# More landing places for the tiles of adj, and the context loaded from GpSimd's queue

## What is computed

```python
h = relu(layernorm(x))
# layer 0: hyperbolic layer; scales per node come from norms of h and of h @ W.T
xt = logmap0(proj(mobius_add(mobius_matvec(W, h), bias)))   # 4096 x 128
s  = adj @ xt                                               # phase 1
x  = x + proj(expmap0(relu(logmap0(proj(expmap0(s))))))
h  = relu(layernorm(x))
# layer 1: attention over the edges of adj
left, right = (context @ W_common.T) @ w_left + b_left, (...) @ w_right + b_right
e = leaky_relu(left[:, None] + right[None, :], 0.2)         # only where adj > 0
x = x + relu(softmax(e) @ h)                                # phase 2
```

## Time and profile before

| | us |
|---|---|
| three runs | 608.92, 609.44, 620.27 |
| median | 609.44 |
| the profiled execution | 609.72 |
| its span | 607.9 |
| start of the first multiplication of phase 1 | 57.84 |
| last copy of the support (phase 1 has ended) | 317.2 |

### The profile page before, as it was taken

How to read it: one execution, slowest core, us unless ns; L and a number is a source line. 1 busy time by engine, 2 the same in 40 slices (tenths; PEclk the granted TensorE clock), 3 DMA queues, 4 the chain that set the end, 5 groups by cost and what they waited for, 6 DMA issues and landing times.

```text
span 607.9 us, 8702 instructions
## 1 busy us (share of the span) xinstructions
PE 500.0 (82%) x2695; PEld 317.0 (52%) x2695; DVE 520.0 (86%) x980; ACT 420.8 (69%) x554; POOL 271.0 (45%) x323
## 2 busy tenths in 40 slices
PE   0731999997999979996984667798989899999995
PEld 0620444332444334432422445687878787887874
DVE  3797898878788788865778999999999999999994
ACT  1965886674757466753658773888888888989871
POOL 4840037989698978672448974201011111111100
PEclk9985999999899989997995788999999999999999
DMA  6999899999999999999950100001010101011010
GB/s 156 218 224 185 156 259 292 299 285 293 245 269 297 278 266 268 295 251 206 269 113 17 36 0 17 20 19 37 18 36 18 35 17 35 17 35 35 0 35 17
DMA packets 157181, 84.59 MB, mean 139 GB/s; under 512 B 7344, under 2 KB 155056, under 8 KB 157152
## 3 DMA queue, kind: packets, MB, share of 16 engines
q1 hardware_dynamic: 88768, 47.20, 35.0%
q10 hardware_dynamic: 65968, 32.65, 23.8%
q0 software_dynamic: 2416, 4.41, 2.7%
HBM read 80.02 MB, written 4.21 MB: 139 GB/s over the span
## 4 chain that ended last, share of the span: by engine, by line
DVE 44%; PE 23%; DMA 15%; issue 11%; ACT 3%; ACTq 1%; POOL 1%; DVEq 1%; SPq 0%; POOLq 0%
PE ps L668 19%; DMA room<-in_adj_dram 14%; DVE room L1132 7%; DVE room L1178 5%; DVE mask L1132 5%; DVE room L1188 4%; DVE room L968 4%; DVE mask L1178 4%; PE ps L694 4%; DVE mask L1188 3%; DVE room L1156 2%; DVE h_room L1202 2%; DMA mask<-in_x_dram 1%; DVE room L1187 1%; ACT mask L826 1%
## 5 line engine op out<-in xcount | busy, mean ns | idle before, releaser
L668 PE MATMUL ps<-room 128*128 128x512 f32 x512 | 239.4, 621 | 37.7 <-DVE room L1057 19.7
L968 DVE STREAM_TRANSPOSE room<-room 128x512 f32<-128x512 f32 x256 | 170.5, 694 | 54.7 <-DMA room<-in_adj_dram 34.2
L826 ACT ACTIVATE mask<-room 128x1024 int8<-128x1024 f32 x128 | 133.4, 1053 | 97.4 <-DVE room L968 94.9
L668 PEld LDWEIGHTS ps<-room 128*128 128x128 f32 x512 | 97.0, 197 | 174.4 <-issue 106.3
L694 PE MATMUL ps<-room 128*128 128x258 f16 x1152 | 142.0, 285 | 32.3 <-DVE room L1188 29.1
L694 PEld LDWEIGHTS ps<-room 128*128 128x128 bf16 x1152 | 115.1, 101 | 58.0 <-DVE room L1188 35.0
L694 PE MATMUL ps<-room,mask 128*128 128x258 f16 x896 | 101.2, 273 | 9.5 <-DVE h_room L1202 6.4
L694 PEld LDWEIGHTS ps<-room,mask 128*128 128x128 bf16 x896 | 86.3, 97 | 23.1 <-DVE h_room L1202 8.1
L879 ACT ACTIVATE room<-mask 128x2048 bf16 (+1 forms) x36 | 68.5, 1903 | 17.1 <-PE ps L694 17.0
L603 POOL TENSOR_TENSOR h_room<-h_room 128x512 f32<-128x512 f32 x7 | 9.8, 1407 | 146.4 <-DVE post L1213 146.4
L452 POOL TENSOR_TENSOR mask<-mask,h_room 128x2048 f32<-128x2048 f32 x8 | 36.3, 4538 | 47.4 <-DVE room L1057 47.1
(11 more groups left out here) (170 smaller groups left out, 563.2 us busy)
## 6 DMA issues: line engine op xcount, KB each, us to landing
room<-in_adj_dram SPq DMA_DIRECT2D x136, 256.0 KB, 8.3
room<-in_adj_dram ACTq DMA_DIRECT2D x120, 256.0 KB, 9.8
mask<-in_L_gnn_context_dram SPq DMA_DIRECT2D x16, 256.0 KB, 11.6
xk<-in_x_dram POOLq DMA_DIRECT2D x32, 64.0 KB, 6.5
out_dram<-xk POOLq DMA_DIRECT2D x32, 64.0 KB, 5.9
h_room<-out_dram SPq DMA_DIRECT2D x32, 64.0 KB, 2.3
out_dram<-h_room SPq DMA_DIRECT2D x28, 64.0 KB, 1.7
mask<-in_x_dram ACTq DMA_DIRECT2D x8, 128.0 KB, 6.3
```

The lines of the kernel that those rows point to most:

```text
L668: pe.matmul(acc[parity], xt[:, k, :], turned[:, k % TSLOTS, :], start=(k == 0), stop=(k == NK - 1)).then_inc(block_multiplied, 1)
L826: nc.scalar.activation(mc[:, half * HB:(half + 1) * HB, :], turned[:, slots:slots + HB, :], ACT.Sign).then_inc(half_signed, 1)
L968: v.transpose(turned[:, k % TSLOTS, :].rearrange("p (l b i) -> p b l i", l=L, b=NQ), loaded[:, g % XSLOTS, :, l * Q:(l + 1) * Q].rearrange ...
```

## The change

The four slots stay, and a list `homes` names further places where a tile may land: two halves of chunk 1's mask, the middle of `h2`, halves of the masks of chunks 4 and 5, and later halves of those of 5, 6 and 7. Each has a first tile, a limit (the tile before which the place is needed for its own purpose) and, for some, a gate: the places in the masks of 4 and 5 may be used after `tangent_scales`, those that the context covers after a part of GpSimd's sums. `give_homes` gives each tile the live place whose last tile is oldest, and `issue_points` says after which tile it is issued. From these lists follows: tiles 0 to 8 need no other tile; tile 9 is issued after tile 0, 10 after 1, 11 after 2, 12 after 3; then each tile t after t-7 (13 to 31). Tiles 31, 32 and 33 are issued after tile 24; 44 and 45 after 37; 54, 55 and 56 after 49. Tiles 61 to 63 are issued after 57 to 59. Tile 33 has the gate `beside_step` >= 36 (parts 3 and 0 done), tile 45 >= 54, tiles 55 and 56 >= 72. The context is issued by GpSimd, after its copy for `w_widened` and before its first load of x.

```diff
-        loaded = view(room, o, [XSLOTS, L * NQ, L * Q], F32)
...
-            assert place[0] >= NK * CH
+            assert place[0] >= 2 * NK * CH
...
+        LAST_TILE = NC * NC
+        AHEAD = 9
+        after_scalars, after_parts = "scalars", ["part 3", "part 0", "part 1", "part 2"]
+        homes = [home(room, XT_BYTES + n * TILE, n, LAST_TILE) for n in range(XSLOTS)]
+        homes += [mask_home(1, 0, 4), mask_home(1, 1, 4), home(h2_room, TILE // 2, 4, 4 * NC + 1)]
+        homes += [mask_home(4, 0, 7, after_scalars), mask_home(5, 1, 7, after_scalars)]
+        homes += [mask_home(5, 0, 4 * NC, after_parts[0]), mask_home(6, 0, 4 * NC, after_parts[1]),
+                  mask_home(6, 1, 45, after_parts[2]), mask_home(7, 0, 55, after_parts[3]),
+                  mask_home(7, 1, 55, after_parts[3])]
...
+        def give_homes():
+            tiles = [[] for _ in homes]
+            home_of, before, use = [], [], []
+            for t in range(LAST_TILE):
+                live = [n for n, (_, first, limit, _) in enumerate(homes) if first <= t < limit]
+                n = min(live, key=lambda n: tiles[n][-1] if tiles[n] else -1)
+                before.append(tiles[n][-1] if tiles[n] else None)
...
+        def gate_of(eng, t):
+            gate = homes[home_of[t]][3]
+            if use_of[t] > 1 or gate is None:
+                return
+            if gate == after_scalars:
+                eng.wait_ge(tangent_scales, 1)
+            else:
+                eng.wait_ge(beside_step, 2 * (after_parts.index(gate) + 1) * SUM_STEPS)
...
-                    if c == 0 and g == XSLOTS - 1:
-                        load_nodes(cx, cx_l, cx_in, range(NQ))
...
-            for c in range(NC):
-                load(c)
+            for t in range(LAST_TILE):
+                gate_of(sp, t)
+                if issue_at[t] >= 0:
+                    sp.wait_ge(block_turned, (issue_at[t] + 1) * L)
+                load_tile(sp, t, LOW if t >= AHEAD else (0, 2, 1, 3))
...
-            sp.wait_ge(block_turned, NC * NK - (XSLOTS - 1) * L)
+            sp.wait_ge(block_turned, (1 + max(t for t in range(LAST_TILE) if home_of[t] == 0)) * L)
...
+            for l in range(L):
+                load_context(l, range(NQ))
...
-                        tile = half // HALVES + XSLOTS
-                        if tile < NC:
-                            load_high(adj_n[c], tile)
-                        elif c < NC - 1:
-                            load_high(adj_n[c + 1], tile - NC)
+                        signed = c * NC + half // HALVES
+                        for t in range(AHEAD, LAST_TILE):
+                            if issue_at[t] == signed:
+                                gate_of(act, t)
+                                load_tile(act, t, HIGH)
```

More of the change, by code:

```diff
@@ L204, in bass_two_graph_layers, with home, mask_home, issue_points @@
         assert NK == Q
+        TILE = L * CH * 4
+        def home(buffer, at, first, limit, gate=None):
+            return view(buffer, at, [L * NQ, L * Q], F32), first, limit, gate
+        def mask_home(c, half, first, gate=None):
+            return home(scratch, c * NK * CH + half * TILE, first, c * NC + half * NC // 2, gate)
+        LAST_TILE = NC * NC
[14 more added lines that the diff above has]
+                before.append(tiles[n][-1] if tiles[n] else None)
+                tiles[n].append(t)
+                home_of.append(n)
+                use.append(len(tiles[n]))
+            return home_of, before, use
+        home_of, before, use_of = give_homes()
+        def issue_points():
+            points, at = [], -1
+            for t in range(LAST_TILE):
+                at = max(at, -1 if before[t] is None else before[t])
+                points.append(at)
+            return points
+        issue_at = issue_points()
+        assert all(at == -1 for at in issue_at[:AHEAD]) and issue_at[AHEAD] >= 0
         ps = ctx.enter_context(nc.psum_tensor("ps", [P, 8, 512], F32))
@@ L220, in bass_two_graph_layers @@
         zeroed, ident_made, powers_made = sem("ident_zeroed"), sem("ident_made"), sem("powers_made")
-        adj_in = [sem(f"adj_loaded_{s}") for s in range(XSLOTS)]
+        adj_in = [sem(f"adj_loaded_{n}") for n in range(len(homes))]
         block_turned, block_multiplied, half_signed = sem("block_turned"), sem("block_multiplied"), sem("half_signed")
@@ L267, in bass_two_graph_layers, with load_tile @@
         adj_n = adj.rearrange("(s r p) (g b j) -> s g b p r j", r=CH // Q, p=Q, b=NQ, j=L * Q)
+        def gate_of(eng, t):
[6 more added lines that the diff above has]
+                eng.wait_ge(beside_step, 2 * (after_parts.index(gate) + 1) * SUM_STEPS)
+        SUM_STEPS = 1 + C.bit_length() - 1
+        def load_tile(eng, t, blocks):
+            for b in blocks:
+                eng.dma_start(homes[home_of[t]][0][b * Q:(b + 1) * Q], adj_n[t // NC, t % NC, b]).then_inc(
+                    adj_in[home_of[t]], 16)
         def pick(view_, c):
@@ L405, in _, with load_context @@
                 pool.dma_start(wlr[:, 2 + n:3 + n], w.broadcast_to([P, 1])).then_inc(context_weights_in, 16)
+            def load_context(l, blocks):
+                for b in blocks:
+                    pool.dma_start(by_l(cx, l)[b * Q:(b + 1) * Q], cx_l[l, b]).then_inc(cx_in[l], 16)
             pool.wait_ge(powers_made, 1)
```

9 lines of the change are left out of this document (3 added, 6 removed).

## The result

| | before | after |
|---|---|---|
| median, us | 610.59 (608.92 to 620.27, 4 runs) | 634.31 (626.66 to 635.7, 4 runs) |
| ratio of the times | | 1.0341, 95% interval 1.0281 to 1.04 |
| profiled run, and its span | 609.72, 607.9 | 634.11, 632.3 |
| last copy of a support, the end of phase 1 | 317.2 | 343.0 |

A forecast was written before the change was run, and what follows sets the result against it. Phase 1 was taken as bound by DMA loads and TensorE, neither with much over: DMA 57.8 + 230.2 + 4.0 + 5.2 = 297.2 us, TensorE 298.2, taken as 299 against 317.2. Hence 18 us less, 591.5 us; range 583 to 606.

The forecast's parts named there:

- DMA path: Loads in phase 1: 66.3 MB after 57.8 us at 288 GB/s take 230.2 us; the path ends at 297.2 us.
- the prediction's own signs of being wrong: Phase 1: rate staying at 225 GB/s after the start, or TensorE's idle time moving from DMA to ScalarE in many places.
- This doesn't cost rate: ScalarE's issues in phase 1: the deeper queue holds ScalarE more, but only while the queue is full, without costing rate.
- the hole: From 57.8 to 68 us, DMA engines nearly resting at 90 GB/s: early released tiles and the context would fill it.
- Rival 4: Phase 1 loads: packets of deep queues stay slow at 225 GB/s, phase 1 ends at 362, total 654 us; chance 0.06.
- The first multiplication: TensorE's start in phase 1: expected at 57.8 us, give or take 1 us.
- The context at no cost and no gain: Context loads in GpSimd's queue, before first use at 86.35 us: zero cost, no gain in the sum.
- The end: Phase 2's first row load waits for block 248 instead of 244: 0 to 1 us; phase 2 keeps its length.
- Rival 3: Before the first multiplication: GpSimd's context issues hold VectorE's scalars; 600 us, or 596 with half; chance 0.16 together with rival 2.
- ScalarE's issues: ScalarE's tile issues in phase 1: longer than the median 0.97 us of before, over 1 us in the median.
- ScalarE at tile 24: Behind tile 24 ScalarE waits for GpSimd's sums: 6.6 us late plus 2.7 restart, 9.3 us on TensorE's path.
- TensorE's path: TensorE's multiplications in phase 1: 285.9 us, plus 3 for GpSimd holding VectorE and 9.3 at tile 24, 298.2 us.

The follow-up runs named there:

- e8: The changed kernel with six places instead of seven: six whole tiles at first, then six ahead up to chunk 4; 609.04 us, ratio 0.999 to the kernel before.
- m1: Tile loads alone, without computation, varying queues, partition halves and tiles out; 194 to 291 GB/s.
- m4: Tile loads alone, with uneven queue limits (290 GB/s) or nine or six whole tiles first in SyncE's queue, some with context and computing engines; about 221, later 289 to 290 GB/s.
- e11: The changed kernel with both queues run nearly empty at tiles 12, 24, 36 and 48, then refilled up to seven ahead; 646.12 us, ratio 1.0538 to the kernel before.
- e13: The changed kernel with the queues run nearly empty only at tile 12; 622.04 us, ratio 1.0121 to the kernel before.
- e14: The changed kernel, lowered at tile 12 only to three tiles ahead, then refilled; 625.91 us, ratio 1.0191 to the kernel before.
- e9: The changed kernel with eight whole tiles at first, then six ahead; 622.56 us, ratio 1.0194 to the kernel before.
- e10: The changed kernel with six whole tiles at first, then seven ahead; 617.2 us, ratio 1.0086 to the kernel before.
- e3: The changed kernel with five places instead of seven (four slots and one in the mask), context in GpSimd's queue; 609.74 us, ratio 0.989 to the kernel before.
- e1: The changed kernel with only the four old slots, so only the context's move to GpSimd's queue remains; 612.34 us, ratio 1.0002 to the kernel before.
- m3: Tile loads alone, seven or four tiles out, with ScalarE work, issues in threes or GpSimd's transfers; 285 to 290 GB/s.
- m2: Tile loads alone, with a lag between the queues (290 GB/s), two whole tiles first (226, then 291) or GpSimd's context DMAs (240, then 290).

## Why the prediction was wrong

It said 591.5 us; 634.3 was measured.

*The step that failed* is the rate in the DMA path: "With up to seven tiles out, instead of four, full slots no longer stop the stream", and "So I take the rate of the deep stretches, 288". It was 236, so that the term of 230.2 us became 280.9, and phase 1 ended at 343 instead of 299. This is also the first of the prediction's own signs of being wrong: the rate stayed at about 225 after the start. The rows of 290 were read as what a deep queue gives. They are one of two states. How the two look, from the queues' shares in single microseconds: first the changed kernel, from 156 and from 158 us, then e8 (six places), from 100 and from 101 us; columns are packets, MB and share (q1 is SyncE's queue, q10 ScalarE's).

```profile
q1 hardware_dynamic: 344, 0.17, 99.3%
q10 hardware_dynamic: 78, 0.04, 23.9%
...
q10 hardware_dynamic: 357, 0.18, 98.1%
q1 hardware_dynamic: 89, 0.04, 24.8%
```

```profile
q1 hardware_dynamic: 285, 0.14, 58.8%
q10 hardware_dynamic: 288, 0.14, 58.5%
...
q10 hardware_dynamic: 292, 0.15, 57.7%
q1 hardware_dynamic: 289, 0.14, 56.1%
```

In the low state the queues take turns: four packets of five are SyncE's, two microseconds later ScalarE's. As each writes its own half of the partitions, one half takes nearly all writes, which m1 measures at 194 to 206 GB/s. At 290 GB/s they go side by side, half and half. An empty queue is not the reason in the kernel: counted from the issues and the packets of the trace, each queue of the changed kernel had two to three and a half DMAs waiting that hadn't begun, from 150 to 160 us. They were less full than where the rate is 290, though: in the mean 2.7 in each from 100 to 160 us, against 3.4 and 3.3 in e8 from 98 to 140. Whether that is cause or effect no run shows. "This doesn't cost rate", said of ScalarE's deeper queue, was the same mistake.

*Why seven places.* Shown is: while whole tiles stand in SyncE's queue the rate is low, and for 9 to 13 us after them (m4), in the changed kernel for all of phase 1; with the queues emptied the low rate ends, at seven places too (e11, e13), and in e14 with three tiles ahead; six whole tiles and six ahead get back to 290, a longer start (e9) or a deeper queue afterwards (e10) costs part of it, and both together all of it. So depth keeps the low state, or lets it come back, rather than being slow in itself. The four slots of the kernel before let the queues run low again and again (a share of 0.37 in the hole at 57.8 us, 1.16 and 1.10 in the dips). That these pauses brought its 290 is argued, not shown, and for the hole, which I wanted to fill, e3 speaks against it: it fills the hole and has 292 all the same.

*Rival 4* named the point, slower below 265 GB/s, which 236 is, and a price of 654 us, at 225 GB/s. Its mechanism, "two loaded queues when their transfers run in step", is near what the shares show, though that they run in turns was not said. Against it stood "83 to 146 us had full queues and 290", the same reading, and so it had 0.06.

*What held.* The hole: 229 GB/s from 57.8 to 68 us, most of it at first the context's (from 56 to 64 us GpSimd's queue moved 1.52 MB of 1.80). The first multiplication: 57.6 us. The DMA engines' work before it: 224 against 219 GB/s. The context at no cost and no gain (e1). By the Trainium skill (DMA: Bandwidth & Descriptors, "Issuing engines are not separate DMA queues") another issuer saves only issue time; for GpSimd's queue e1 agrees, with its ratio of 1.0002, and for SyncE's and ScalarE's m1 doesn't, with 290 against 206 and 223. The end: phase 2 within 1.4 us. Rival 3 did not come: VectorE was busy for 36.36 us before the first multiplication, against 36.19, while GpSimd issued.

*ScalarE's issues.* A median of over 1 us was expected. For ScalarE it is 0.51 us over all of its tiles, less than the 0.97 of before; it is SyncE whose issues grew, to 2.10 us in the median from 0.54. ScalarE's were long where it asked for several tiles in a row.

*ScalarE at tile 24.* A stop of 6.6 us and one restart were expected, with GpSimd as releaser. TensorE stood still for 7.22 us there, and ScalarE for 10.24. But the chain has three issues of ScalarE in it, 170.95 to 177.74, and GpSimd's part was done at 171.25: the full queue held it, which I had costed at nothing because ScalarE was to be held only while it didn't matter. It comes again at 229.84 to 236.37. From 146 to 176 us the rate is 236 GB/s all the same, as in the stretch before, so in a phase whose length the loads set I count no further loss.

*TensorE's path*, 298.2 us, was never the bound and stays unmeasured. That the two paths would end together within 1 us was never put to the test.

*What stays open:* what makes the queues take turns, whether their being less full is part of it, and what brings the state back (in e10 and e13 it returns in chunks 3 to 5; GpSimd's transfers, which m3 shows to be harmless by themselves, are near, but not shown to be the cause). Whether six or seven places would gain if the first tiles were split over both queues from the start wasn't tried.

## What to carry to other kernels

Before a deeper prefetch is costed at the best rate of the trace, ask what the rate is made of: the same busy share can hold 206, 223 and 290 GB/s, and here it depended on whether both halves of the partitions were written at once. Here two queues that never ran low kept the low state through a whole phase, and with seven tiles ahead the one of 290 only for some 60 us (e10, e13). One place more than before gained 1.7% (1.1 to 2.3), two more nothing, three more cost 3.4%. And look at each issuer's queue in single microseconds, not only at the sum.

## What the runs showed of the hardware that I had not expected

- One queue with DMAs over all 128 partitions: 291 GB/s; with DMAs over 32 partitions, 223 when the halves alternate, and 206 in one half (m1).
- Two queues with a half each run at 290 or, in turns of about two microseconds, at 211 to 222, with the same share of 1.20 to 1.22. The low rate lasted 9 to 13 us after the whole tiles had landed (m4), and all of phase 1 with seven tiles ahead.
- A queue whose DMA comes to engines that another queue has loaded waits: in m2 its first packet came 4.5 and 4.7 us after the issue, against 1.0 to 1.9 us where both began at once.
- A full queue holds the issuing engine for about as long as a DMA takes to leave: 2.04 us in the median for SyncE, 2.1 to 2.3 for ScalarE at tile 24, where the shortest issues take 0.31 and 0.32.
